# Second half of a cross attention with two tiles under way, and routing by top-8 instructions in four groups, in a decoder layer on one core

## The reference

```
x = x + attention(layernorm(x))        # 16 heads of 128, mxfp4 weights
x = x + cross(layernorm(x), ctx)       # 16 heads, latent keys and values of 64
x = x + moe(layernorm(x))

# cross, for each sequence:
scores = einsum('bhsr,bhlr->bhsl', q_r, k_r);  attn = softmax(scores)
ctx_c  = einsum('bhsl,bld->bhsd', attn, kv_r);  out = heads(ctx_c, w_kc_kv) @ Wo.T

# moe: 16 experts in 4 groups of 4; 2 groups are taken, then 4 experts in them
scores = softmax(xt @ Wg.T)
gidx = top_k(scores.reshape(T, 4, 4).max(-1), 2)[1]
topi = top_k(where(gmask, sg, -inf).reshape(T, 16), 4)[1]
y = sum over the 4 experts of weight * (silu(xt @ W1.T) * (xt @ W3.T)) @ W2.T
z = silu(xt @ Ws1.T) * (xt @ Ws3.T) @ Ws2.T        # shared experts, all tokens
out = y + z
```

## Time and profile before

| | |
|---|---|
| time before, three runs | 737.15, 734.08, 729.28 us; median 734.08 |
| the profiled execution | 736.92 us, of it 735.5 us span |
| busy in the span | PE 606.1 us (82%), DVE 397.9 (54%), ACT 254.8 (35%), POOL 203.2 (28%) |
| second half of the cross attention, from the scores of tile 4 to the end of tile 7's output | 417.8 to 517.6 us |
| from there to the first block's transposes | 517.6 to 580.5 us |
| blocks and end | 580.5 to 735.5 us |

### The profile page before, as it was taken

How to read it: one execution, slowest core, us unless ns; L and a number is a source line. 1 busy time by engine, 2 the same in 40 slices (tenths; PEclk the granted TensorE clock), 3 DMA queues, 4 the chain that set the end, 5 groups by cost and what they waited for, 6 DMA issues and landing times. The chain is left out here.

```text
span 735.5 us, 10537 instructions
## 1 busy us (share of the span) xinstructions
PE 606.1 (82%) x3729; PEld 488.0 (66%) x3729; DVE 397.9 (54%) x853; ACT 254.8 (35%) x516; POOL 203.2 (28%) x171
## 2 busy tenths in 40 slices
PE   7789999999997999989999974763766389899970
PEld 6678978988886956656667653642665268787860
DVE  3477556365346486765577339533447175443436
ACT  2245355355253301031121243222303166454540
POOL 3525400200001032243343203282007223333340
PEclk9999999999999999999999987886868599999995
DMA  8999330035999690000000220010302463232317
GB/s 268 242 234 217 75 143 1 15 142 123 238 206 213 163 234 4 0 1 1 0 1 0 98 95 0 30 57 30 135 1 80 146 239 88 78 92 86 94 26 286
DMA packets 41106, 76.93 MB, mean 105 GB/s; under 512 B 4823, under 2 KB 27999, under 8 KB 40800
## 3 DMA queue, kind: packets, MB, share of 16 engines
q1 hardware_dynamic: 19616, 49.64, 23.2%
q10 hardware_dynamic: 17648, 18.18, 12.1%
q0 software_dynamic: 3792, 8.43, 3.3%
HBM read 66.76 MB, written 28.48 MB: 129 GB/s over the span
## 5 line engine op out<-in xcount | busy, mean ns | idle before, releaser
L1191 DVE TENSOR_TENSOR tt<-psum,tab 128x512 f32<-128x512 f32 x96 | 60.3, 681 | 23.7 <-PE psum L623 22.9
L1566 POOL DMA_INDIRECT parts_of_tokens<-yb,xg x47 | 46.3, 985 | 94.0 <-ACT yb L1029 91.4
L799 PE MATMUL psum<-EW,xgh 128*128 x188 | 59.0, 356 | 4.4 <-issue 4.2
L492 PE MATMUL psum<-xTh,W 128*128 128x512 f32 x128 | 52.8, 413 | 7.4 <-ACT qT L865 3.9
L641 PE MATMUL psum<-rp,Mb 128*128 128x512 f32 x128 | 58.0, 597 | 0.6 <-DVE rp L1216 0.5
L1533 POOL TENSOR_TENSOR rp<-tt,tt 128x512 f32<-128x512 f32 x24 | 30.7, 1280 | 96.2 <-DVE tt L1191 96.2
L1419 DVE TENSOR_TENSOR xgl<-psum,xgh 128x256 fp32r<-128x256 f32 x47 | 19.9, 423 | 68.1 <-ACT xgh L1011 66.9
L1161 DVE TENSOR_TENSOR OTl<-psum,OTh 128x512 fp32r<-128x512 f32 x32 | 22.1, 691 | 54.8 <-ACT OTh L898 54.8
L492 PE MATMUL psum<-xTl,W 128*128 128x512 f32 x128 | 51.7, 404 | 0.0
L1560 POOL DMA_INDIRECT rows_of_experts<-xe,posi x32 | 33.8, 1057 | 59.3 <-DVE posi L1344 50.6
L623 PE MATMUL psum<-xTh,Ah 128*128 128x512 f32 x96 | 42.0, 437 | 2.0 <-DVE tt L1191 2.0
(11 more groups left out here) (226 smaller groups left out, 1605.0 us busy)
## 6 DMA issues: line engine op xcount, KB each, us to landing
rows_of_experts<-in_empty ACTq DMA_DIRECT2D x7, 2064.0 KB, 22.2
exr<-in_ex SPq DMA_DIRECT2D x16, 608.0 KB, 5.6
xg<-rows_of_experts SPq DMA_DIRECT2D x47, 129.0 KB, 2.1
raw<-in_codes SPq DMA_DIRECT2D x4, 1024.0 KB, 19.2
sclB<-in_scl SPq DMA_DIRECT2D x16, 256.0 KB, 11.1
yv<-parts_of_tokens SPq DMA_DIRECT2D x8, 512.0 KB, 7.2
rows_of_experts<-in_empty ACTq DMA_DIRECT2D x1, 2193.0 KB, 24.8
raw<-in_codes SPq DMA_DIRECT2D x4, 512.0 KB, 17.0
```

Source lines behind the costliest of these rows:

```text
L492: mm = pe.matmul(ap, W[:, kt, m, 512 * hq + 128 * h:512 * hq + 128 * h + 128], xp[:, kt, 512 * g:512 * g + 512], start=(n == 0), stop=(n = ...
L799: mm = pe.matmul(ap[:, 0:352], xp[b % 2][:, 128 * kt:128 * kt + 128], EW[:, bass.ds(weights[b] + (o + 352 * kt), 352)], start=(k == 0), st ...
L1191: return tt_(b3(tt[n][:, :], 64), b3(src, 64), tab[:, j % 3, n, :].unsqueeze(1).to_broadcast([128, 8, 64]), ALU.mult)
L1566: nc.gpsimd.indirect_dma_start(out=parts_of, out_offset=to, in_=yb[b % 4][:, :], in_offset=None, bounds_check=4 * 1024 - 1, oob_is_err=Fal ...
```

## The change

1. `second_half()` takes the place of `cross_order(1, early_order(), ...)`. A second buffer `sm2` and PSUM banks 4 and 5 let odd tiles be scored while even ones are worked on: the scores of t+2 are issued on PE behind the values of t. Beside the tiles stand the routing of tiles 0 to 3 (group 0), its 16 indirect DMAs, the routing and the 8 indirect DMAs of tiles 4 and 5 (group 1), and experts 0 to 3. No shared tile is done there.
2. Routing goes in groups of 4, 2, 1 and 1 tiles (`GROUPS`). The logits come out of PE untransposed (6 matmuls of 16 columns for each tile). Two levels of `max` (the 8 largest in a row) and `max_index`, one instruction each for each tile and level, replace the comparisons of all pairs. A running sum `cum` replaces most matmuls of `rank`: two for each tile, and one more for the total.
3. `last_routes()` takes the place of `late_order()`: all 8 shared tiles stand after the cross attention; groups 2 and 3 (tiles 6 and 7) are routed beside shared tiles 0 and 1; the DVE part of a shared tile (`mix`) is now a step of its own behind the turn of the tile before, with two banks each for the turned and the last products.
4. The low parts of experts 0 to 3, 7, 8, 10, 12 and 14 (`BY_POOL`) are made by POOL, that of expert 4 and the others by DVE.
5. The addition of 1e-5 in `norm` is a `tensor_tensor` with a constant column in place of a `tensor_scalar`.

The core of the diff (left out: the other uses of the second buffer and banks, the buffers' places, `dispatch`, and the old functions, which the listing above shows):

```diff
+BY_POOL = (0, 1, 2, 3, 7, 8, 10, 12, 14)
+GROUPS = ((0, 4), (4, 2), (6, 1), (7, 1))
...
+def routing(n):
+    t0, some = GROUPS[n]
+    return ([("logits", n)] + [("route", n, k) for k in range(3)] + [("rank", n), ("dispatch", n)]
+            + [("scatter", t) for t in range(t0, t0 + some)])
+def second_half():
+    first, pair = routing(0), routing(1)
+    beside = {4: ([("copies", 0), ("copies", 1), ("expert", 0)] + first[:2], first[2:3] + [("expert", 1)]),
+              5: ([("copies", 2), ("copies", 3)] + first[3:6], first[6:] + [("expert", 2), ("expert", 3)]),
+              6: ([("copies", 4)], pair[:2]),
+              7: ([("copies", 5)] + pair[2:], routing(2)[:1])}
+    yield from [("cross_scores", 4), ("cross_exp", 4), ("cross_scores", 5)]
+    for t in range(4, 8):
+        yield from [("cross_norm", t, 0), ("cross_norm", t, 1), ("cross_turn", t)]
+        if t < 7:
+            yield ("cross_exp", t + 1)
+        yield ("cross_values", t)
+        if t < 6:
+            yield ("cross_scores", t + 2)
+        if t > 4:
+            yield ("norm_turn", 2, t - 1)
+        yield from beside[t][0]
+        yield from [("cross_out", t), ("norm", 2, (t,))]
+        yield from beside[t][1]
+def last_routes():
+    six, seven = routing(2), routing(3)
+    yield from [("widen",), ("hidden", 0), ("copies", 6)] + six[1:2] + [("norm_turn", 2, 7), ("mix", 0)]
+    yield from seven[:1] + [("copies", 7)] + six[2:3] + [("turn_hidden", 0), ("turn_low", 0)] + seven[1:2]
+    yield from [("hidden", 1)] + six[3:5] + seven[2:3] + six[5:] + seven[3:5] + [("mix", 1)] + seven[5:]
+    yield from [("table", 0), ("down", 0), ("add_shared", 0)]
+    for t in range(2, 8):
+        yield from [("hidden", t), ("turn_hidden", t - 1), ("turn_low", t - 1), ("mix", t)]
+        if t == 2:
+            yield ("table", 1)
+        yield from [("down", t - 1), ("add_shared", t - 1)]
+        if t > 2:
+            yield ("expert", t + 1)
+    yield from [("turn_hidden", 7), ("turn_low", 7), ("down", 7), ("add_shared", 7)]
...
-                sides = [ps.place(2 + n, "cs", t, n) for n in range(2)]
+                b = 2 + (2 * (t % 2) if t >= 4 else 0)
+                sides = [ps.place(b + n, "cs", t, n) for n in range(2)]
                 for n in range(2):
-                    te.wait_ge(ps.drained[2 + n], sides[n][1])
+                    te.wait_ge(ps.drained[b + n], sides[n][1])
                 for hp in range(8):
...
-                    ts_(bst[:, t % 4, 7:8], bst[:, t % 4, 7:8], 1e-5, None, ALU.add).then_inc(s_var, 1)
+                    ve.wait_ge(s_half, 2)
+                    tt_(bst[:, t % 4, 7:8], bst[:, t % 4, 7:8], eps[:, :], ALU.add).then_inc(s_var, 1)
...
                 if t == 0:
                     ve.wait_ge(s_pb, 16)
                     ve.wait_ge(s_pb_pool, 2)
+                elif t <= 4:
+                    ve.wait_ge(*ps.filled("ct", t - 1, 1))
+                elif t == 5:
+                    ve.wait_ge(*ps.emptied("lat", 1, 7))
                 else:
-                    ve.wait_ge(*ps.filled("ct", t - 1, 1))
-                less_max(16 + 2 * t, "cs", t)
+                    ve.wait_ge(*ps.filled("ct", t - 2, 1))
+                less_max(16 + 2 * t, sm_of(t), "cs", t)
```

348 lines of the change are left out of this document (123 added, 225 removed).

## The result

| | kernel before | changed kernel |
|---|---|---|
| beside each other | 733.18 us, 4 runs (729.28 to 737.15) | 740.04 us, 4 runs (739.3 to 743.75) |
| once more, later | 731.66 us, 17 runs (724.38 to 740.77) | 739.43 us, 6 runs (734.45 to 742.34) |
| profiled execution, its span | 736.92 us, 735.5 us | 739.98 us, 738.7 us |
| busy in the span | PE 606.1 us, DVE 397.9, POOL 203.2 | PE 611.3 us, DVE 390.6, POOL 214.6 |

The changed kernel takes 1.0121 times the time of the kernel before (95% interval 1.0072 to 1.017), and 1.0143 times (1.0094 to 1.0193) in the second measurement. The forecast was 734.4 us, no change, in a range of 719 to 749 us. The time lies in the range, 5.6 us above the forecast, and inside the 727 to 741.5 us that I had called within 1%; the ratios are a little over 1%, and 1% lies in both intervals.

A forecast was written before the change was run, and what follows sets the result against it. No engine was full; chains of short steps bound the kernel. About 13 us later at tile 7, 11 less to the blocks and 2 less there gave +0.3 us on the profiled 736.92, hence 734.4 us against the median, range 719 to 749.

The forecast's parts named there:

- POOL's queue: Cross attention, between the roots of tiles 5 and 6: 16 indirect DMAs and two low parts on POOL, 26.0 us.
- Softmax, values, lock: Cross attention tiles: softmax 3.2 us, values 3.78 at the low clock, 2.8 added where POOL's EW blocks tile 4's xh.
- Top-8 instructions: Routing on DVE: max taken at 0.2 us and max_index at 0.3, four of each 2.0 us.
- The rival that they are dear: Routing on DVE: max and max_index at the upper bound, 9 us slower, 743 us; chance 0.07.
- the one that they are cheap: Routing: max and max_index at their lower bound and the lock missed, 6.5 us faster, 728; chance 0.12 with part of high clock.
- The output behind a rank: Cross attention on PE: a tile's output takes 3.69 us, also where it follows the 3.4 us rank of tiles 0 to 3.
- To the turned tile 7: End of cross attention: the turned tile 7 (xTl) is ready 1.4 us behind its xh at 532.9.
- DVE's row: Behind tile 7's xh: turn, routing of tiles 6 and 7 and two mixes in one row on DVE, 13.8 us, to 546.7.
- Shared periods: Shared tiles 2 to 7 on PE: 5.0 us a period, near the high clock, last product ending at 582.8.
- The rival of eight shared tiles at the low clock: Shared tiles after cross attention: periods of 7.35 us in place of 5.0, 745 us in all; chance 0.13.
- Blocks: From the last product on: no wait for rows -1.8 us, warm start -0.9, POOL's low parts delaying an indirect DMA +0.7.
- The lock in the blocks: Blocks: POOL's and DVE's low parts exclude each other and POOL's indirect DMAs wait, up to +8.4 us, 742; chance 0.06.

The follow-up runs named there:

- e1_split: Changed kernel with POOL's indirect DMAs split behind the norms of tiles 5, 6 and 7, expert 3's low part moved along: 724.06 us, 0.9845 of the kernel before.
- e4_one_tile: Changed kernel with scores and exponentials of the next tile only after the norm of the current one, one tile under way: 740.22 us, ratio 1.0096 to before.
- e5_after_again: The changed kernel, unedited, run and profiled once more: 739.43 us over 6 runs, ratio 1.0143 to the kernel before.
- e2_logits_first: Changed kernel with tile 6's logits and the first part of their routing ahead of tile 7's output: 735.62 us, ratio 1.0039 to the kernel before.
- e6_spread: Changed kernel with the routing of tiles 6 and 7 spread over the shared experts' periods: 743.33 us, ratio 1.0171 to the kernel before.
- e9_low_by_dve: Changed kernel with the low parts of experts 7, 8, 10, 12 and 14 back from POOL to DVE: 739.99 us, ratio 1.009 to before.
- e8_warm: Changed kernel with sixteen unread transposes in PE's waits ahead of the ranks of tiles 0 to 3 and 4 and 5: 742.21 us, ratio 1.0131 to before.

## Why the prediction was right or wrong

Positions are those of the changed kernel's profiled execution. Its cross stage starts 1.15 us later than that of the profile of before (tile 4's first maxima at 420.17 against 419.02), for no reason that lies in the change.

- **POOL's queue: right, and it was the point.** Forecast 26 us from root to root and a wait of 11 us at tile 6: 26.95 and 11.41. At tile 7 forecast 7, measured 5.08. e1_split shows that this costs 13 to 16 us, and e4_one_tile that two tiles under way gain nothing behind it.
- **Softmax, values, lock: right.** Values 3.75 us (3.78 taken), the lock 2.4 us (2.8 taken), logits of four tiles 2.7 us (2.6 taken).
- **Top-8 instructions: taken too dear, with no consequence.** The first part of the routing took 2.7 us in place of 4.0. Independent `MAX8` follow each other after 0.07 to 0.08 us, and `MATCH_VALUE_LOAD` with `FIND_INDEX8` after 0.13, where my lower bound was 0.14 for each. The rival that they are dear is refuted; of the one that they are cheap, the lock was there, and 1.3 us were left.
- **The output behind a rank: mis-sized, in this profile by 3.0 and 2.3 us.** I took 3.69 us from the earlier trace rows, where the output stands behind 3.78 us of values. There it began at PE's high level, 379 ns for a matmul. In the new order the output of tiles 5 and 7 stands behind a wait of 5.1 us and a `rank`, and most of its matmuls are at the low level, 634 to 774 ns: 6.69 and 6.02 us. I priced values by the clock and the output not. How much of it is at the low level varies: in the other profile of the same kernel (e5_after_again) the two take 5.04 and 5.17 us, 1.4 and 1.5 more than I took. Set against what came cheaper, it makes the root of tile 6 the 1.2 us later that remain after the start is taken off, and the `xh` of tile 7 1.4 us.
- **To the turned tile 7: the step that failed.** Forecast 1.4 us behind `xh`, measured 6.4. Here I took the turn of tile 7 as the next thing on PE and had the hidden of shared tile 0 done beforehand. It could not be: it needs the bank of the logits of tile 6, which DVE empties only behind the `xh` of tile 7, because its row has `norm` of tile 7 ahead of `route(2, 0)`. I had followed each engine's waits and not the banks, which the diff moves too. e2_logits_first shows the 5 to 6 us of it.
- **DVE's row: right.** From the end of `xTl` of tile 7 to the end of `mix` 1 10.7 us (541.88 to 552.55); forecast 12.4 from 534.3 to 546.7. The last indirect DMA is issued at 559.75 and SP fetches the first rows at 563.51, where I had the DMAs done and the first fetches near 557; the blocks begin at 588, so nothing hangs on that. That it would be better spread over the periods was my own expectation in e6_spread, and wrong.
- **Shared periods: right.** 4.76 us, forecast 5.0, at a granted clock near 1 from 560 on. The rival of eight shared tiles at the low clock (7.35 us) is refuted. (The parts that I named add up to 4.6 and 7.4, not 4.65 and 7.35, and the rows that I named for tile 5's maxima give 2.57 us where I wrote 2.7 and 2.66 was measured; neither matters to the sum.)
- **Blocks.** Their start behind the last product, without a wait for rows: as forecast. The first six matmuls start 2.2 us behind it (590.17; I had 1.5) and take 1.24 us against 2.14 before, the 0.9 that I had. From the last product to the end 150.7 us, forecast 153.0. In the profiles of the variants this stage takes between 150 and 156 us, so that the 2.3 us are within what varies. The lock in the blocks: there, 2.00 us in place of 0.97 on three indirect DMAs, but with DVE's `EW` as its partner where I had POOL's own stand ahead of them, and worth nothing (e9_low_by_dve).
- **The sum.** Forecast for the last product 582.8, measured 587.98: 1.15 from the start, 1.4 from the output at the low level less what was cheaper, 5.0 from the bank, and 2.4 back from a shorter row and shorter periods. With 2.3 less in the blocks the profile ends 2.9 us later than I had it. The rest of the 5.6 us is the reference: the profiled execution of before lay 2.8 us above its median and I carried that difference over, while that of the changed kernel is equal to its own median.

So the time came out within 0.8% of the forecast, in part by luck: the 5.0 us of the bank, which I had not seen, were nearly paid back by 2.4 and 2.3 us of terms taken too dear, the second of which is within what the stage of the blocks varies. And "no change" was still a little off: the bank alone, 5 to 6 us, is about what separates the two. None of the rivals on the slower side is what happened.

## What to carry to other kernels

An instruction of half a microsecond that another engine waits for must not stand behind a burst of indirect DMAs: count what each in-order queue, POOL's and ACT's as much as PE's, has ahead of every step that the long chain needs, and put work with slack behind it. Where a change puts work side by side, follow the PSUM banks as well as the semaphores, since who empties a bank, and behind what, decides as much as who fills it. And free time of an engine that is part of every period's chain is no place for extra work: pay it once, outside the periods.

## What the runs showed of the hardware

- The sixteen matmuls of an output take 3.70 us (379 ns each, overlapping) at tile 4 and 6.69 us (up to 774 ns each) at tile 5 of the changed kernel, and 5.04 us at tile 5 in its other profile. Less than 1 us ahead of the fast ones stand values, scores or logits; ahead of the slow ones a wait of 5.1 us and a `rank`, of 3.4 us at tile 5 and 1.7 at tile 7. In e8_warm it was 1.9 us of transposes, 3.3 us of waiting and the rank, and the output was slow too.
- On DVE a `MAX8` over 8 or 16 elements takes 0.07 to 0.08 us of the time in a row of independent ones, a `MATCH_VALUE_LOAD` with its `FIND_INDEX8` 0.13 to 0.14 us; in the chain of dependent instructions of 1 to 16 elements behind `xTl` of tile 7 (from 543.04 on) each starts 0.20 us behind the one before, a `MAX8` as well as a sum, and only that pair takes 0.28.
- An indirect DMA on POOL mostly repeats after 1.27 to 1.28 us in every kernel of this study, 16 in a row as well as 8. It takes 2.00 us where a DVE `EW` (two inputs in SBUF) began ahead of it and still runs, and 0.99 us where it comes 0.17 us behind an `EW` of POOL itself (496.41 before) or begins ahead of DVE's (599.92, DVE's `EW` at 599.96, in the changed kernel).
- A DVE cast of 8 elements took 2.79 us beside POOL's `EW`: the lock does not look at how small the instruction is. The Trainium skill (SBUF — State Buffer, Who interferes with whom) lists casts among those that can take the shared ports, and this row agrees.
